# Block-diagonal ones: stacking two halves on 64 partitions so that one matmul does the work of two

## The reference, cut to what matters

```
xn = layernorm(x)                                   # x: (8, 2048, 2048), one row of 2048x2048 a core
Q, K, V = xn @ W_q, xn @ W_k, xn @ W_v              # 16 query heads, 4 key/value heads, head size 128
Qr, Kr  = rope(Q), rope(K)
weights = softmax(Qr Kr^T / sqrt(128))
attn    = (weights @ V) @ W_o
gate = silu((xn @ w_gate) * s_gate); up = (xn @ w_up) * s_up      # int8 weights, inner size 8192
ffn  = ((gate * up) @ w_down) * s_down
out  = x + attn + ffn
```

## Time and profile before

| what | value |
|---|---|
| timed runs of the kernel before | 3490.6, 3573.27, 3616.72 us; median 3573.27 |
| profiled execution, its own time | 3487.79 us |
| its span (slowest core, core 7) | 3486.1 us |
| spans of the eight cores | 3471.1 to 3486.1 us |
| mean granted TensorE clock | 0.995 to 0.996 |
| busy in the span | PE 3399.9, DVE 2391.4, ACT 1205.7, POOL 1624.7 us |

### The profile page before, as it was taken

One profiled execution on the slowest core, in us unless ns is written; L12 is line 12 of the kernel. 1 busy time (PEld: TensorE's weight loads), 2 busy tenths in 40 slices (PEclk: granted clock), 3 DMA queues, 4 the chain that ended last, 5 costly groups with the idle time before them and its releaser, 6 DMA issues.

```text
span 3486.1 us, 49034 instructions; the slowest of 8 cores (3471.1 to 3486.1 us)
## 1 busy us (share of the span) xinstructions
PE 3399.9 (98%) x15824; PEld 1542.6 (44%) x15824; DVE 2391.4 (69%) x3226; ACT 1205.7 (35%) x1437; POOL 1624.7 (47%) x1521
## 2 busy tenths in 40 slices
PE   5899999999999999999999999999999999999999
PEld 2444444444444444444444444444444444444444
DVE  5468777767776777677743677677776777677633
ACT  4421133443334333443311133443344333433111
POOL 1134445555555555555511155555555555555311
PEclk9999999999999999999999999999999999999999
DMA  8555476698668776667697666676667666676864
GB/s 214 156 114 145 152 209 181 169 151 170 181 179 144 155 191 178 143 143 195 183 225 124 145 180 184 150 169 176 183 153 164 176 181 154 142 183 181 210 127 85
DMA packets 180568, 578.98 MB, mean 166 GB/s; under 512 B 28256, under 2 KB 54880, under 8 KB 176096
## 3 DMA queue, kind: packets, MB, share of 16 engines
q0 software_dynamic: 132768, 484.53, 60.2%
q1 hardware_dynamic: 47552, 91.32, 8.2%
HBM read 318.64 MB, written 109.05 MB: 123 GB/s over the span
## 4 chain that ended last, share of the span: by engine, by line
PE 89%; DMA 4%; DVE 3%; issue 2%; ACT 1%; POOL 1%; DVEq 0%; POOLq 0%; ACTq 0%; SPq 0%
PE ps_f L109 54%; PE ps_f L113 8%; PE ps_s L109 7%; PE ps_av L109 6%; PE ps_k L109 4%; PE ps_s L113 3%; PE ps_av L113 3%; PE ps_m L109 2%; DMA x_t<-x_nat 1%; DMA wab<-wd 1%; PE ps_m L113 1%; DMA outT<-ost 1%; DVE st L368 1%; POOL kst L473 0%; ACT expT L990 0%
## 5 line engine op out<-in xcount | busy, mean ns | idle before, releaser
L109 PE MATMUL ps_f<-xop,wab 128*128 128x512 bf16 x6272 | 1545.2, 379 | 15.4 <-DVE th L750 7.1
L990 ACT ACTIVATE expT<-ps_s,bias,isq_sb 128x1024 bf16<-128x1024 f32 x512 | 616.6, 1204 | 1092.9 <-PE ps_s L113 1043.3
L1007 POOL TENSOR_TENSOR acc<-acc,expT 128x1024 f32<-128x1024 f32 x320 | 688.5, 2152 | 634.9 <-ACT expT L990 581.4
L109 PEld LDWEIGHTS ps_f<-xop,wab 128*128 128x128 bf16 x6272 | 612.1, 98 | 761.2 <-issue 28.2
L109 PE MATMUL ps_f<-fop,wab 128*128 128x512 bf16 x3136 | 770.8, 380 | 12.9 <-DVE fop L766 4.5
L109 PEld LDWEIGHTS ps_f<-fop,wab 128*128 128x128 bf16 x3136 | 306.8, 98 | 386.4 <-issue 19.6
L113 PE MATMUL ps_f<-xop,wab 128*128 128x512 bf16 x896 | 339.6, 379 | 0.0
L814 DVE TENSOR_TENSOR ps_f<-ps_f,usum 128x512 f32<-128x512 f32 x384 | 264.8, 690 | 72.1 <-PE ps_f L113 64.9
L791 ACT ACTIVATE ost<-ps_f,sd_sb 128x512 f32<-128x512 f32 x256 | 174.5, 686 | 306.6 <-DVE ps_f L814 195.4
L822 DVE TENSOR_TENSOR usum<-usum,ps_f 128x512 f32<-128x512 f32 x384 | 260.0, 677 | 13.3 <-PE ps_f L113 13.1
L745 ACT ACTIVATE th<-ps_f,sgh 128x512 f32<-128x512 f32 x256 | 170.4, 686 | 229.5 <-DVE ps_f L814 194.9
(11 more groups left out here) (116 smaller groups left out, 3782.9 us busy)
## 6 DMA issues: line engine op xcount, KB each, us to landing
wab<-wg POOLq DMA_DIRECT2D x299, 512.0 KB, 4.9
wab<-wu POOLq DMA_DIRECT2D x296, 512.0 KB, 4.9
wab<-wd POOLq DMA_DIRECT2D x146, 512.0 KB, 4.8
outT<-ost POOLq DMA_DIRECT2D x127, 512.0 KB, 7.7
x_t<-x_nat SPq DMA_DIRECT2D x16, 1024.0 KB, 9.2
wo_sb<-wo POOLq DMA_DIRECT2D x32, 512.0 KB, 9.4
ring<-wq POOLq DMA_DIRECT2D x16, 512.0 KB, 7.8
q_scr<-kst SPq DMA_DIRECT2D x64, 128.0 KB, 2.8
```

The lines of the kernel that those rows point to most:

```text
L109: streams["t"].append(lambda t, o=out, l=lhsT, r=rhs, a=start, z=stop: t.matmul(o, l, r, start=a, stop=z, skip_group_check=True))
L990: e = op("s", lambda s, kk=k, gg=g, rr=r, tt=t: s.activation(expT[:, kk, :], ps_s[:], AF.Exp, bias=bias[:, gg, rr, tt:tt + 1], scale=isq_s ...
L1007: summed = op(eng, lambda x, d=acc, o=one, kk=k: x.tensor_add(d[:], o, expT[:, kk, :]))
```

## The change

Two places are changed in the same way.

For the softmax total, the sum is kept on 64 partitions. `fold` on GpSimd still adds the two column halves of `acc` at step 7. Then `shift` (ScalarE, step 1 of the next tile) copies partitions 64 to 127 of the folded sum to partitions 0 to 63, beside it. `split` (GpSimd, step 2) adds the two, writes the bfloat16 part to `hl[0:64]` and the remainder to `lo[0:64]`. `lower` (ScalarE, step 3) copies `lo` to `hl[64:128]`. `total` at step 4 is one matmul with `ones` over `hl`. The endings after the last tile take six steps in place of three, so `STEPS` is 263.

For the query norms, ScalarE squares each tile in two instructions of 64 partitions (`sqb` and `squ`), two tiles side by side in the partitions, GpSimd adds `squ` onto `sqb` after every second tile, and one matmul with `halves` (ones in two diagonal blocks of 64 by 64) gives the norms of both tiles, the one on the upper and the other on the lower partitions. One reduction serves two tiles. `finish_norms` copies the result apart into `qmaxs` with four small VectorE copies.

```diff
--- before.py
+++ after.py
@@ -28,7 +28,7 @@
 UNITS = 96
 LEAD = 80
 LAST = 87 * 56 - 28
-STEPS = 260
+STEPS = 263
 NEG_CBOUND = -1.02 / (2.0 * math.sqrt(128.0))
 INV_SQRT_HD = 1.0 / math.sqrt(128.0)
 
@@ -132,6 +132,7 @@
 
         KB = 1024
         ones = place("ones", [128, 128], BF16)
+        halves = place("halves", [128, 128], BF16)
         sgh = place("sgh", [128, IC], F32)
         sgu = place("sgu", [128, IC], F32)
         sd_sb = place("sd_sb", [128, DC], F32)
@@ -159,6 +160,7 @@
         rpa = [place("rpa%d" % i, [128, TS], F32, a_sm + 4 * KB * i) for i in range(2)]
         rpb = [place("rpb%d" % i, [128, TS], F32, a_sm + 4 * KB * i + 2 * KB) for i in range(2)]
         sqb = [place("sqb%d" % i, [128, TS], BF16, a_sm + 8 * KB + KB * i) for i in range(2)]
+        squ = [place("squ%d" % i, [128, TS], BF16, a_sm + 12 * KB + KB * i) for i in range(2)]
         kst = [place("kst%d" % i, [128, TS], BF16, a_sm + 10 * KB + KB * i) for i in range(2)]
         vst = [place("vst%d" % i, [128, TS], BF16, a_et + KB * i) for i in range(2)]
         at = [a_et + 2 * KB]
@@ -177,6 +179,7 @@
         eps_sb = small("eps_sb", [128, 1])
         spare = small("spare", [128, 2])
         qmaxs = small("qmaxs", [128, G, H // G, NT])
+        qmax2 = small("qmax2", [128, G, H // G, 2])
         st6 = [small("st6_%d" % i, [128, 4, 6]) for i in range(2)]
         mv = [small("mv%d" % i, [128, 2, 2]) for i in range(2)]
         std = [small("std%d" % i, [128, 2]) for i in range(2)]
@@ -196,7 +199,7 @@
         th = [place("th%d" % i, [128, TS], F32, a_et + 8 * KB + 2 * KB * i) for i in range(4)]
         acc_0 = place("acc_0", [128, 2 * TS], F32, a_sm)
         acc_1 = place("acc_1", [128, 2 * TS], F32, a_sm + 4 * KB)
-        hi = place("hi", [128, TS], BF16, a_sm + 8 * KB)
+        hl = place("hl", [128, TS], BF16, a_sm + 8 * KB)
         lo = place("lo", [128, TS], BF16, a_sm + 9 * KB)
         av_sb = place("av_sb", [128, TS], F32, a_sm + 10 * KB)
         ao = [place("ao%d" % i, [128, TS], BF16, a_sm + 12 * KB + KB * i) for i in range(2)]
@@ -321,6 +324,9 @@
 
 
         op("g", lambda g: g.memset(ones[:], 1.0))
+        wait("g", op("g", lambda g: g.memset(halves[:], 0.0)))
+        for k in (0, 64):
+            wait("g", op("g", lambda g, k=k: g.memset(halves[k:k + 64, k:k + 64], 1.0)))
         op("g", lambda g: g.memset(eps_sb[:], 1e-5))
         consts = op("g", lambda g: g.memset(isq_sb[:], INV_SQRT_HD))
         id_loaded = dma("g", l_id, lambda g: g.dma_start(ident[:], idd))
@@ -438,9 +444,9 @@
 
             def norms(left):
                 while len(behind) > left:
-                    squared, k, dst = behind.pop(0)
+                    squared, k, dst, within = behind.pop(0)
                     wait("t", squared, m_free[0])
-                    summed = mm_last(ps_m[:], ones[:], sqb[k][:], True, True)
+                    summed = mm_last(ps_m[:], within[:], sqb[k][:], True, True)
                     sq_free[k] = summed
                     wait("v", summed)
                     m_free[0] = op("v", lambda v, d=dst: v.reduce_max(d, ps_m[:], axis=AX.X))
@@ -465,12 +471,23 @@
                 op("v", lambda v: v.tensor_mul(rpa[r][:], bank[:], cos_sb[t][:]))
                 op("v", lambda v: v.tensor_mul(rpb[r][0:64, :], bank[64:128, :], sin_sb[t][0:64, :]))
                 freed = op("v", lambda v: v.tensor_mul(rpb[r][64:128, :], bank[0:64, :], sin_sb[t][64:128, :]))
-                wait("s", freed, sq_free[r])
-                squared = op("s", lambda s: s.activation(sqb[r][:], bank[:], AF.Square))
-                behind.append((squared, r, biggest))
+                if n < G:
+                    wait("s", freed, sq_free[r])
+                    squared = op("s", lambda s: s.activation(sqb[r][:], bank[:], AF.Square))
+                    behind.append((squared, r, biggest, ones))
+                else:
+
+                    k, at_ = (n * NT + t) // 2 % 2, t % 2 * 64
+                    wait("s", freed, sq_free[k])
+                    op("s", lambda s: s.activation(sqb[k][at_:at_ + 64, :], bank[0:64, :], AF.Square))
+                    squared = op("s", lambda s: s.activation(squ[k][at_:at_ + 64, :], bank[64:128, :], AF.Square))
                 bank_free[b] = (squared,)
                 wait("g", freed, st_free[r])
                 rp_free[r] = op("g", lambda g: g.tensor_add(kst[r][:], rpa[r][:], rpb[r][:]))
+                if n >= G and t % 2:
+                    wait("g", squared)
+                    both = op("g", lambda g: g.tensor_add(sqb[k][:], sqb[k][:], squ[k][:]))
+                    behind.append((both, k, biggest, halves))
                 wait("y", rp_free[r])
                 st_free[r] = dma("y", l_kst[r], lambda y: y.dma_start(dst, kst[r][:]))
                 return done
@@ -574,7 +591,7 @@
                     (XP7, xn[0], HB, xn[1], HB, ALU.add)]
             for h in range(H):
                 for t in range(NT):
-                    done = rotated(G + h, t, qscr[h, t], qmaxs[:, h % G, h // G, t:t + 1])
+                    done = rotated(G + h, t, qscr[h, t], qmax2[:, h % G, h // G, t // 2:t // 2 + 1])
                 proj.release(G + h, done)
                 if h == 0:
                     xop_ready.append(op("s", lambda s: s.activation(X[:, X11], xn[0][:, 0:HB, :], AF.Copy)))
@@ -612,6 +629,11 @@
             def finish_norms():
                 norms(0)
                 wait("v", m_free[0])
+                for t in range(2):
+                    for k in (0, 64):
+                        last = op("v", lambda v, a=64 * t, t=t, k=k: v.tensor_copy(
+                            qmaxs[k:k + 64, :, :, t::2], qmax2[a:a + 64]))
+                wait("v", last)
                 kmax_ready = op("v", lambda v: v.reduce_max(kmax[:], kmaxs[:], axis=AX.X))
                 wait("v", kmax_ready)
                 for g in range(G):
@@ -945,21 +967,35 @@
                 av_free[0] = op("s", lambda s: s.activation(av_sb[:], ps_av[:], AF.Copy))
                 return av_free[0]
 
-            def split(j, acc, summed):
-
+            def fold(acc, summed):
                 wait("g", summed)
-                f = op("g", lambda g: g.tensor_add(acc[:, 0:TS], acc[:, 0:TS], acc[:, TS:]))
+                return op("g", lambda g: g.tensor_add(acc[:, 0:TS], acc[:, 0:TS], acc[:, TS:]))
+
+
+
+            def shift(c):
+                acc = c["acc"]
+                wait("s", c["sum"])
+                c["sum"] = op("s", lambda s: s.activation(acc[0:64, TS:], acc[64:128, 0:TS], AF.Copy))
+
+            def split(c):
+                acc = c["acc"]
+                wait("g", c["sum"])
+                f = op("g", lambda g: g.tensor_add(acc[0:64, 0:TS], acc[0:64, 0:TS], acc[0:64, TS:]))
                 wait("g", f, hl_free[0])
-                f = op("g", lambda g: g.tensor_copy(hi[:], acc[:, 0:TS]))
+                f = op("g", lambda g: g.tensor_copy(hl[0:64, :], acc[0:64, 0:TS]))
                 wait("g", f)
-                acc_free[j % 2] = op("g", lambda g: g.tensor_sub(lo[:], acc[:, 0:TS], hi[:]))
-                return acc_free[j % 2]
+                c["low"] = acc_free[c["j"] % 2] = op("g", lambda g: g.tensor_sub(
+                    lo[0:64, :], acc[0:64, 0:TS], hl[0:64, :]))
+
+            def lower(c):
+                wait("s", c["low"], hl_free[0])
+                c["parts"] = op("s", lambda s: s.activation(hl[64:128, :], lo[0:64, :], AF.Copy))
 
             def total(c):
 
                 wait("t", c["parts"], m_free[0])
-                mm(ps_m[:], ones[:], hi[:], True, False)
-                hl_free[0] = mm_last(ps_m[:], ones[:], lo[:], False, True)
+                hl_free[0] = mm_last(ps_m[:], ones[:], hl[:], True, True)
                 invert(c, 0)
 
             def invert(c, half):
@@ -975,7 +1011,7 @@
                 wait("y", avs_free[0])
                 ao_free[j % 2] = dma("y", l_ao[j % 2], lambda y: y.dma_start(ascr[t, :, h, :], ao[j % 2][:]))
 
-            ending = {4: total, 5: lambda c: invert(c, 1), 6: normalise}
+            ending = {1: shift, 2: split, 3: lower, 4: total, 5: lambda c: invert(c, 1), 6: normalise}
             for j in range(32):
                 g, r, t = j // 8, j % 8 // 2, 2 * p + j % 2
                 q, b = qr[j % 2], g % 2
@@ -1009,7 +1045,7 @@
                         if i == 1:
                             exp_used[(k + 3) % 4].append(summed)
                     if i == 7:
-                        summed = split(j, acc, summed)
+                        summed = fold(acc, summed)
                     if ahead is not None:
                         av_done = weigh()
                         if ahead[1] == 7:
@@ -1018,7 +1054,7 @@
                         load_kv(g + 1)
                     ahead = (j, i, e)
                     if i == 7:
-                        pending = dict(parts=summed, j=j)
+                        pending = dict(sum=summed, j=j, acc=acc)
                     yield
```

## The result

| | before | after |
|---|---|---|
| profiled execution | 3487.79 us | 3468.81 us |
| median of the undisturbed timed runs | 3490.05 us | 3469.4 us |
| ratio, 95% interval | | 0.9942 [0.9922, 0.9961] |

The change is 0.6% faster, some 20 us, and so within 2%.

The account below looks back on a forecast made before the run. TensorE's queue was taken as the bound: -20.7 us for removed matmuls, +1.2 at the last norm and +8 in the passes make -11.5 from the profiled 3487.8, so 3476 us; range 3455 to 3580.

Parts of the forecast that it names:

- The bound: Whole kernel: TensorE's queue sets the time, busy 98% of the span; other engines matter only when late at a bank.
- the price of a matmul: TensorE: each costs its distance to the next, 0.2158 us; 64 attention and 32 query matmuls removed give -20.7 us.
- The query stage: Query norms: split squares cost ScalarE 1.2 us a tile, GpSimd's addition 1.26 per two tiles, all covered, so no cost.
- The last norm: End of the prologue: TensorE waits longer for the second square and GpSimd's addition, +1.2 us once.
- The hand-offs: Passes, steps 1 to 4: shift, split, lower, total have slack, 2.7 us typical and 0.1 tightest, so lower never waits.
- I take +8 us: Passes: added ScalarE copies (4 us) and moved GpSimd splits (3.5 us) push other work late; bounds -5 and 77 us.
- one in twenty: Passes: 28.3 us of idle time in some 30 places over 512 steps, so roughly one step in 20 has no slack.
- the bound at -5: Passes: lower bound of the pushing-about term, with GpSimd freed by 1.9 us at step 7 and gaps closing.
- the first (gaps close): Passes: rival with free hand-offs and closing gaps, -24.5 us in all, 3463 us; chance 0.27.
- The port: Step 2: rival where GpSimd's additions block VectorE on shared SBUF access, 0.6 us a tile, 38 us, 3507 us; chance 0.14.
- nothing would be given back: TensorE: rival where shortened stretches end in the next wait, 3488 us within 3 us; chance 0.12.

Follow-up runs that it names:

- two_mm: Changed kernel with the 96 removed matmuls put back as repeats, all added work kept; ratio 1.0006 to the kernel before, 4.9 us slower.
- phase_261: Kernel before with one empty attention step at the end of a pass, STEPS 261; ratio 0.9988, 1.9 us faster than before.
- phase_263: Kernel before with three empty attention steps at the end of a pass, STEPS 263; ratio 1.0019, 11.2 us slower than before.
- late_261: Changed kernel, norms finished after 40 instead of 8 feed-forward matmuls, six last endings in four steps, STEPS 261; ratio 0.9929 to the kernel before, 22.1 us faster.
- tight: Changed kernel with shift, split and lower all at step 3, total still at step 4, STEPS 261; ratio 1.0410 to the kernel before, 144.8 us slower.
- moved_split: Kernel before with hi and lo made at step 2 instead of 7, 128 partitions, both matmuls kept, STEPS 261; ratio 1.0001, 5.9 us faster by medians.

## Why the prediction was right or wrong

**The bound** and **the price of a matmul**: right. 23.0 us for 96 of them in two_mm, 19.5 us of PE busy time, 20.7 forecast.

**The query stage**: ScalarE's 1.2 us a tile was right (2 x 0.59), so was GpSimd's addition (1.15 for 1.26). "Nothing is paid here" was off by 1 to 2 us of waits for banks (2.3 on the slowest core). **The last norm**: +1.2 us forecast, 3.21 against 2.01 measured; that the clock falls behind the longer wait, 1.7 us on most cores, the sum had not.

**The hand-offs**: right in mechanism. A slack of 2.7 us in a typical tile and 0.1 in the tightest was read off the kernel before, and the wait for `lo` is 4.0 us in all, at two tiles. Full time for 64 partitions was right. In its new place beside VectorE's addition GpSimd's part took even 0.4 us a tile more, so that its busy time rose by 136 us, just over the 85 to 130 given.

**The step that failed** is the last of that part, "I take +8 us" for the pushing about. The passes lost nothing: idle went from 27.9 us to between 22 and 25 at the median core, and the clock took up to 1.7 us of that back, so the term was -3 to -4 and not +8, and that is most of what lies between 11.5 us forecast and some 20 measured. With it the sum closes: -20.7 for the matmuls, +1.2 and some 1.4 of clock at the last norm, 1 to 2 in the query stage, -3 to -4 in the passes make a gain of 19 to 21 us, where 18 to 21 were measured. The argument was a chance for each added instruction to hit a bank without slack, one in twenty. The runs put two things in its place. The waits aren't spread by chance: they stand at fixed places which the spacing of the steps sets, and I had passed over 263 for 260 as a reshuffling, although a spacing can be worth more than the whole term (phase_261 and phase_263 differ by 13 us). And the relief of step 7, which I had kept for the bound at -5, was of that size by the medians, 4 to 6 us. The first dose of added work cost nothing that could be measured; a second of 161 to 200 us cost 14 to 18 us, so one in twenty fits the second dose and not the first. How the three combine to the -3 to -4 of the changed kernel stays open: their single prices (+11, -4 to -6, 0 or below) don't add up to it, and late_261 shows that the price of a spacing doesn't carry over.

**The number itself** failed in its basis too, and in microseconds this is the larger step. 3476 was made against the profiled 3487.8, a change of -0.3%. Beside the median then shown, 3573.3, it reads as -2.7%, a gain that no step of the sum has and that the text itself excluded (0.96 for within 2%). The range's upper end had the same cause. The measured time of 3469 lies in the range.

**The rivals**: the first (gaps close) was nearest in mechanism, since idle time shrank. It had 0.27 where the forecast had 0.47; in time, 3469 lies halfway between its 3463 and the forecast's 3476. That it lies inside the forecast's 3468 to 3484 is luck, since the term of +8 has the wrong sign. The port showed its sign, the longer VectorE addition at step 2, but a loss came only when GpSimd's work was raised further, and even if all of it is the port's, it is 0.2 to 0.3 us a tile, the rival's point of decision and not its 0.6. That nothing would be given back is refuted by two_mm.

## What to carry to other kernels

Where one engine is busy 98% of the time, price its instructions by their pitch and expect that back; before pricing the work moved to other engines, follow the hand-offs tile by tile in the timeline, and spread them over as many steps as there are, since the same work made TensorE wait nowhere over three steps and cost 2.5 us a tile in one. Look at the granted clock behind the longest waits as well: nearly half of what a spacing cost here was in no idle time. Where steps are mixed into another stream by a count, that count is a term of its own: run the old kernel with the new count and no other change before explaining a difference of half a percent. A first dose of work can be free and the second not, so test with more of it before calling an engine idle enough.

## What the runs showed of the hardware that was not expected

GpSimd takes as long on 64 partitions as on 128. The same addition of 512 float32 columns, on 64 and on 128 partitions, in tight, where both run mostly alone (durations in ns: least, median, most):

```profile
L984 POOL TENSOR_TENSOR acc<-acc x64: 1253/1259/1829, 509.4 to 3384.7; 64x512 f32<-64x512 f32 x64
L972 POOL TENSOR_TENSOR acc<-acc x64: 1262/1274/1558, 491.9 to 3382.3; 128x512 f32<-128x512 f32 x64
```

That the averages in the kernel after are higher comes from the place at step 2 and not from the 64 partitions. The cast to `hi` on all 128 partitions, at step 7 in the kernel before and at step 2 in moved_split, shows it:

```profile
L953 POOL CAST hi<-acc x64: 609/610/1421, 495.3 to 3243.2; 128x512 bf16<-128x512 f32 x64
L957 POOL CAST hi<-acc x64: 622/917/1157, 502.9 to 3226.3; 128x512 bf16<-128x512 f32 x64
```

ScalarE took 0.59 us for a square of 64 x 512 from PSUM, against 0.60 for 128 x 512, and 0.63 us for a copy of 64 x 512 from SBUF to the other half of the partitions.

TensorE's clock fell from full to 0.50 for some 3.4 us behind single waits: of 3.2 us at the last norm, and of 2.4 us on core 0 of tight, which ended at 1093.81 us and behind which the windows from 1095 to 1097 us show 0.50. Not every wait of that length had it: the 62 waits of that core for `hl` reach 3.2 us, and fourteen such stretches show in its passes.
